# Experts' tiles in the order in which batches begin them, results added while later tiles run, and layer 0's maxima piece ahead of the scores

## What is computed

```python
xn = _layernorm(x)
x = x + _L0_attn_ref(xn, ...) + _L0_ffn_ref(xn, ...)      # 16 heads of 8, |i-j| <= 128
xn = _layernorm(x)
x = x + _L1_attn_ref(xn, ...) + _L1_ffn_ref(xn, ...)      # one head of 128; 8 experts, top 2
```

```python
scores_topk, idx = jax.lax.top_k(xn @ w_router.T, 2)
up = moe_linear(xf, ids, w_up); u, gate = jnp.split(up, 2, axis=-1)
down = moe_linear(u * silu(gate), ids, w_down)
out = jnp.sum(down.reshape(B, S, 2, D) * weights[..., None], axis=-2)
return out + skip
```

## Time and profile before

| | |
|---|---|
| median of 3 runs | 628.71 us (627.55 to 628.91) |
| the profiled execution, its own time | 624.67 us |
| its span | 622.9 us |
| PE busy | 528.2 us (85%) |
| DVE busy | 445.0 us (71%) |
| ACT busy | 359.2 us (58%) |
| POOL busy | 293.0 us (47%) |
| mean DMA rate | 98 GB/s |

### The profile page before, as it was taken

One profiled execution on the slowest core, in us unless ns is written; L12 is line 12 of the kernel. 1 busy time (PEld: TensorE's weight loads), 2 busy tenths in 40 slices (PEclk: granted clock), 3 DMA queues, 4 the chain that ended last, 5 costly groups with the idle time before them and its releaser, 6 DMA issues. The chain is left out here.

```text
span 622.9 us, 17045 instructions
## 1 busy us (share of the span) xinstructions
PE 528.2 (85%) x5698; PEld 308.3 (49%) x5698; DVE 445.0 (71%) x1868; ACT 359.2 (58%) x1073; POOL 293.0 (47%) x327
## 2 busy tenths in 40 slices
PE   5389999899998999989999669998976999999940
PEld 4124454444444444444444436655654666666630
DVE  7698898797887979878890169999881664455526
ACT  4504777767677676776677357677641444444420
POOL 6661836447164471641000026877871555555540
PEclk9555999999999999999999779999978999999985
DMA  3946073462734627246001273111121222222229
GB/s 98 185 104 136 26 170 86 120 138 67 156 74 119 139 66 161 53 121 137 21 20 26 62 258 99 42 46 49 44 87 52 65 75 75 78 75 77 79 73 359
DMA packets 50837, 60.99 MB, mean 98 GB/s; under 512 B 9905, under 2 KB 41781, under 8 KB 48960
## 3 DMA queue, kind: packets, MB, share of 16 engines
q1 hardware_dynamic: 45280, 49.34, 32.3%
q0 software_dynamic: 4320, 8.47, 4.0%
q10 hardware_dynamic: 1152, 2.10, 0.9%
HBM read 31.68 MB, written 28.39 MB: 96 GB/s over the span
## 5 line engine op out<-in xcount | busy, mean ns | idle before, releaser
L639 DVE CUSTOM_DVE_ANT_0 A<-A,band 128x320 f32<-128x320 f32 (+2 forms) x512 | 214.4, 465 | 43.8 <-PE A L801 42.7
L502 ACT ACTIVATE Pb<-SB 128x320 f32<-128x320 f32 (+2 forms) x512 | 174.9, 402 | 84.8 <-PE SB L837 82.7
L801 PE MATMUL A<-Ks,Qs 48*64 48x320 bf16 (+2 forms) x1024 | 131.3, 307 | 9.2 <-DVE mneg L639 3.7
L828 PE MATMUL SB<-Qs,Ks 50*64 50x320 bf16 (+2 forms) x1024 | 125.9, 292 | 12.6 <-ACT Pb L502 10.8
L828 PEld LDWEIGHTS SB<-Qs,Ks 50*64 50x64 bf16 x1024 | 55.8, 106 | 102.3 <-ACT Pb L502 85.2
L1577 POOL DMA_INDIRECT results<-y,xt x71 | 69.5, 979 | 62.3 <-ACT y L1591 56.6
L837 PE MATMUL SB<-ends,ident 64*64 64x64 bf16 (+1 forms) x1024 | 97.5, 205 | 0.0
L850 PE MATMUL PV<-Pb,Va 128*32 128x320 f32 (+2 forms) x1024 | 85.6, 406 | 0.4 <-ACT Pb L502 0.4
L1677 PE MATMUL l_S<-w_up,xT 128*128 x142 | 77.7, 629 | 1.4 <-ACT xT L1585 1.4
L639 DVE DVE_READ_ACCUMULATOR2_ANT mneg<- 128x1 f32 x512 | 72.7, 142 | 0.0
L1133 POOL DMA_INDIRECT expert_rows<-pay,pos x64 | 62.9, 983 | 19.4 <-issue 18.2
(11 more groups left out here) (229 smaller groups left out, 912.7 us busy)
## 6 DMA issues: line engine op xcount, KB each, us to landing
Qs<-parts_dram SPq DMA_DIRECT2D x16, 384.0 KB, 5.9
Ks<-parts_dram SPq DMA_DIRECT2D x16, 384.0 KB, 9.2
xt<-expert_rows SPq DMA_DIRECT2D x71, 65.0 KB, 1.8
yb<-results SPq DMA_DIRECT2D x8, 512.0 KB, 6.9
parts_dram<-qp SPq DMA_DIRECT2D x16, 192.0 KB, 2.9
parts_dram<-kp SPq DMA_DIRECT2D x16, 192.0 KB, 2.8
xb<-in_x SPq DMA_DIRECT2D x8, 256.0 KB, 2.8
parts_dram<-qp SPq DMA_DIRECT2D x16, 128.0 KB, 2.6
```

Of the source, the lines that this page charges most:

```text
L502: act.activation(Pb[:, group % 4, c, 0:w], SB[k % NB_BANKS][:, 0:w], ACT.Exp).then_inc(act_exp, 1)
L639: nc.vector.tensor_tensor_reduce(scores_of, scores_of, band[:, skip:skip + w], -1.0, 3e38, ALU.add, ALU.min, mneg[:, step % 2, col:col + 1 ...
L801: mm = nc.tensor.matmul(A[k % NA_BANKS][out:out + HP, 0:w], Qs[b % RING][rows, a, HP * sub:HP * sub + HP], Ks[b % RING][rows, a, lo:lo + w ...
L828: nc.tensor.matmul(out[r0:r0 + HP, 0:w], Ks[b % RING][rows, a, HP * sub:HP * sub + HP], Qs[b % RING][rows, a, lo:lo + w], start=True, stop ...
```

## The change

Three things are changed.

1. In layer 0, PE's loop issues `piece` before `scores` in every unit, and four side jobs move: `turn_xq` from u = 46 to 48 and its copy from 47 to 49, `turn_max` from 52 to 53 and its copy from 53 to 54.
2. The table of tiles orders them by the batch in which an expert's tile gets its first row, then by expert. For this PE keeps a count of each expert's rows after every batch (one more matmul of 8 columns in `rank`), DVE computes the table in 128 partitions (partition t for tile t) from 64 (batch, expert) cells, PE turns the two columns, and DVE copies them to `tab`. DVE prepares constants for it in batch 6 (`order_constants`).
3. A batch's results are loaded, added and stored while later tiles run. SP loads `yb` of batch b after `load(22 + 8 b)` for b up to 6, DVE adds it in tiles 22 + 8 b and 23 + 8 b for b up to 5, and SP stores it after `load(30 + 8 b)`. Only batch 7's load, and the adding and storing of batches 6 and 7, come after the tiles.

By count: an expert's tiles begun by batches 0 to b number at most 8 (b + 1) + 7 in all, so they lie among tiles 0 to 8 b + 14, and `load(22 + 8 b)` has waited for the results of just these.

```diff
@@ layer0, ACT @@
-                if u == 53 and b + 1 < NB:
+                if u == 54 and b + 1 < NB:
                     evac_mT(STEPS * b + 2)
...
-                    if u == 47:
+                    if u == 49:
                         evac_xqT(g)
@@ layer0, PE @@
             for u in range(SLOTS):
-                scores(b, u)
                 step, n = ahead(STEPS * b + u // UNITS, u % UNITS)
                 if step < NSTEP:
                     piece(step, n)
+                scores(b, u)
...
-                if u == 52 and b + 1 < NB:
+                if u == 53 and b + 1 < NB:
                     turn_max(STEPS * b + 2, (act_xqT, g + 1) if g < NB else (dve_x1, b))
...
-                    if u == 46:
+                    if u == 48:
                         turn_xq(g, (dve_x1, b) if b > 0 else (act_k1, g))
@@ layer1, DVE @@
+        def order_constants():
+            nc.vector.tensor_copy(tile_f[:], tile_i[:]).then_inc(dve_const, 1)
+            nc.vector.tensor_scalar(tile_row[:], tile_i[:], float(P), None, ALU.mult).then_inc(dve_const, 1)
+            nc.vector.tensor_tensor(upto[:], ..., ALU.is_le).then_inc(dve_const, 1)
...
         def tables():
...
+            step(nc.vector.tensor_tensor(more[:], now, before, ALU.subtract))
+            step(nc.vector.tensor_tensor(cprod[:], upto[:].unsqueeze(1).to_broadcast([P, NB, NE, NE]),
+                                         more[:].unsqueeze(2).to_broadcast([P, NB, NE, NE]), ALU.mult))
+            step(nc.vector.tensor_reduce(cwithin[:], cprod[:], AX.X, ALU.add), False)
...
+        def rows_of_tiles():
+            dve.wait_ge(pe_cols, 1)
+            step(nc.vector.tensor_copy(tab[:], QK[0:1, 0:2 * P].rearrange("p (c t) -> p c t", t=P)[:, :, 0:NTILES]))
...
             if not last:
                 ranks(g, last)
+            if g == NB - 2:
+                order_constants()
...
             nc.vector.tensor_tensor(x2b[:, g * NT:(g + 1) * NT, :], OU[:].rearrange("p (i d) -> p i d", i=NT),
                                     xn[g % 3][:], ALU.add).then_inc(dve_out, 1)
+        rows_of_tiles()
@@ layer1, PE @@
+            if g > 0:
+                c = CNT + NE * (g - 1)
+                mm = nc.tensor.matmul(RT[:, c:c + NE], ones[:], S[p][:], start=True, stop=True)
             mm.then_inc(pe_rank, 1)
...
+        pe.wait_ge(dve_fin, COLS)
+        pe.wait_ge(act_k, NB)
+        for c in range(2):
+            mm = nc.tensor.transpose(QK[0:1, c * P:(c + 1) * P], sums[:, c:c + 1], ident[:])
+        mm.then_inc(pe_cols, 1)
         pe.wait_ge(dve_fin, FIN)
@@ experts @@
+    READY = NE * 2 + 6
+    SUM_AT = READY
+    SENT_AT = READY + 8
...
+    def store(engine, b):
+        engine.wait_ge(dve_done, b + 1)
+        engine.dma_start(ov[b], x2b[:, b * NT:(b + 1) * NT, :].rearrange("p i d -> p (i d)")).then_inc(stored, 16)
@@ experts, SP @@
             load(t)
+            if t >= READY and (t - READY) % NE == 0:
+                results((t - READY) // NE)
+            if t >= SENT_AT and (t - SENT_AT) % NE == 0:
+                store(sp, (t - SENT_AT) // NE)
         for r in range(R):
             sp.wait_ge(dma_y[r], 16 * turns(r))
-        for b in range(NB):
-            sp.dma_start(yb[:, b].rearrange("p i k d -> p (i k d)"), yv[b]).then_inc(dma_yb[b], 16)
+        results(NB - 1)
@@ experts, ACT @@
-        for b in range(NB):
-            act.wait_ge(dve_done, b + 1)
-            act.dma_start(ov[b], ...).then_inc(stored, 16)
+        for b in range(NB - 2, NB):
+            store(act, b)
@@ experts, DVE @@
+            if t >= SUM_AT and t < SUM_AT + NE * (NB - 2):
+                if (t - SUM_AT) % NE == 0:
+                    both((t - SUM_AT) // NE)
+                if (t - SUM_AT) % NE == 1:
+                    total((t - SUM_AT) // NE)
         turned(NTILES - 1)
...
+        for b in range(NB - 2, NB):
+            both(b)
+            total(b)
```

More of the change, by code:

```diff
@@ L956 @@
 CAP = TOKENS + P
+NCELL = NB * NE
 NTILES = (TOKENS * TOPK + NE * (P - 1)) // P
@@ L1047, in layer1 @@
     padi = sb("padi", [1, NE], I32)
[L1048 to L1059 removed]
+    nt_a = sb("nt_a", [P, NCELL])
+    nt_f = sb("nt_f", [P, NB + 1, NE])
+    more = sb("more", [P, NB, NE])
+    cprod = sb("cprod", [P, NB, NE, NE])
+    cwithin = sb("cwithin", [P, NB, NE])
+    cbefore = sb("cbefore", [P, NB])
+    cum = sb("cum", [P, NB, NE])
+    back = sb("back", [P, NB, NE])
+    base = sb("base", [P, NCELL + 1])
+    bstep = sb("bstep", [P, NCELL])
+    le = sb("le", [P, NCELL])
+    steps = sb("steps", [P, 2, NCELL])
+    sums = sb("sums", [P, 2])
     Sb, XR, QK, OU = banks
     XV, RT = XR[:, 0:512], XR[:, 512 + 2 * (P + NE):1024]
+    CNT = 64
     blocks = XR[:].rearrange("p (b w) -> p b w", b=2)[:, :, 0:2 * (P + NE)].rearrange("p b (i w) -> p b i w", i=2)
@@ new lines, in tables @@
+            step(nc.vector.tensor_reduce(cwithin[:], cprod[:], AX.X, ALU.add), False)
+            step(nc.vector.tensor_reduce(cbefore[:], before, AX.X, ALU.add))
+            step(nc.vector.tensor_tensor(cum[:], cwithin[:], cbefore[:].unsqueeze(2).to_broadcast([P, NB, NE]), ALU.add))
+            step(nc.vector.tensor_tensor(back[:], now, cum[:], ALU.subtract))
+            step(nc.vector.scalar_tensor_tensor(base[:, 0:NCELL].rearrange("p (b e) -> p b e", e=NE), back[:], float(P),
+                                                ebase[:].unsqueeze(1).to_broadcast([P, NB, NE]), ALU.mult, ALU.add))
@@ L1516, in _ @@
         pe.wait_ge(act_exp, NT * NB)
-        pe.wait_ge(act_k, NB)
         pe.wait_ge(dve_rb, RB * NB)
@@ L1623, in residual, with both, total @@
             nc.vector.tensor_tensor(rows, rows, xall[:, b], ALU.add).then_inc(dve_res, 1)
+        def both(b):
+            dve.wait_ge(dma_yb[b], 16)
+            nc.vector.tensor_tensor(yb[:, b, :, 0, :], yb[:, b, :, 0, :], yb[:, b, :, 1, :], ALU.add).then_inc(dve_sum, 1)
+        def total(b):
+            rows = x2b[:, b * NT:(b + 1) * NT, :]
+            dve.wait_ge(dve_sum, b + 1)
+            dve.wait_ge(dve_res, b + 1)
+            nc.vector.tensor_tensor(rows, yb[:, b, :, 0, :], rows, ALU.add).then_inc(dve_done, 1)
         for t in range(NTILES):
@@ L1633, in dve_part @@
                 residual(t - FIRST_RES)
-        turned(NTILES - 1)
-        dve.wait_ge(dve_res, NB)
-        for b in range(NB):
-            dve.wait_ge(dma_yb[b], 16)
-            rows = x2b[:, b * NT:(b + 1) * NT, :]
-            nc.vector.tensor_tensor(yb[:, b, :, 0, :], yb[:, b, :, 0, :], yb[:, b, :, 1, :], ALU.add).then_inc(dve_sum, 1)
-            dve.wait_ge(dve_sum, b + 1)
-            nc.vector.tensor_tensor(rows, yb[:, b, :, 0, :], rows, ALU.add).then_inc(dve_done, 1)
+            if t >= SUM_AT and t < SUM_AT + NE * (NB - 2):
[3 more added lines that the diff above has]
+                    total((t - SUM_AT) // NE)
+        turned(NTILES - 1)
+        for b in range(NB - 2, NB):
+            both(b)
+            total(b)
     def pe_part(pe):
```

93 lines of the change are left out of this document (41 added, 52 removed).

## The result

| | kernel before | with the change |
|---|---|---|
| median | 628.81 us (623.52 to 631.59, 12 runs) | 625.08 us (622.32 to 629.12, 12 runs) |
| ratio, 95% interval | | 0.9945 (0.992 to 0.9969) |
| profiled execution, its own time | 624.67 us | 624.18 us |
| span | 622.9 us | 622.4 us |

What follows compares the result with a forecast made beforehand. No engine full in layer 0, PE pacing the tiles, uncovered transfers bounding the end. Terms -11.2 - 4.0 - 2.0 + 0.5 = -16.7 us: 608.0 from the profiled 624.67, 612.0 as a median; range about 604 to 620.

Steps and rivals of the forecast that it cites:

- The end: After the tiles: only batch 7's load, additions and store remain, 7.75 us instead of 18.91, a gain of 11.2 us.
- The shorter load alone: At the end: batch 7's load, with none behind it, might take 1.8 us instead of 3.90, making the gain 13.3.
- Layer 0: Layer 0: moved side jobs -4.0 us and `piece` ahead of `scores` -2.0 us.
- The moves: Layer 0: `l_x1s` is asked for later, so PE's wait at the turning of `xq` goes, 5 times 0.8, -4.0 us.
- the swap: Layer 0: `piece` ahead of `scores` shortens DVE's waits for PE, -2.0 us; upper bound 8, loss bounded by 2.
- layer 0 gives nothing: Rival, chance 0.20: in layer 0 PE's wait goes but another engine is next at once; 618.0 us.
- The slower rival: Layer 0, chance 0.05: PE's waits for DVE's maxima delay ACT's exp; at 0.04 us a unit, 20.5 us, giving 634.5.
- The table: Between layer 0 and the tiles: the new table's work is covered by about 4 us before the first tile; zero cost.
- The side effect: Before the first tile: PE idles about 2 us instead of 3.67; a higher clock could return at most 1.6, taken as 0.
- The tiles: Expert tiles: seven `yb` loads in SP's queue delay xt loads little, +0.5 us in all, bounds 0 and 5.5.
- the rival of held loads: Expert tiles, chance 0.20: xt loads wait behind `yb` and `out` in SP's queue, 5.5 us instead of 0.5; 617.0 us.
- The additions: Expert tiles: DVE's two additions of 0.69 us per batch, in two tiles, cost nothing while PE sets the pace.

Runs made afterwards that it cites:

- both_on_act: The changed kernel with the same `yb` loads and `out` stores, back to back, issued by ACT instead of SP, sum four tiles behind `yb`: 658.68 us, ratio 0.9946.
- ring_11: The changed kernel with 11 instead of 8 buffers of xt and y, `yb` three tiles later, batches 6 and 7 loaded behind the tiles: 615.33 us, ratio 0.9815.
- l0_both_only: The kernel before with only the layer 0 part: `piece` ahead of `scores` and the four side jobs moved: 657.75 us, ratio 0.9941.
- the mended kernel: The changed kernel with 11 buffers of xt and y, `yb` in four parts, stores in two halves: 645.17 us, ratio 0.9753; run again 650.18 us, 0.982.

## Why the prediction was wrong

**The end: right.** -11.2 forecast, 11.2 found, and 7.55 us from the last load for 7.75. The shorter load alone, kept as an end of the range, was not seen: 3.70 us with nothing behind it, for 3.90.

**Layer 0: right in sum, wrong in its parts.** -6.0 forecast; the seven batches gave 4.3 to 6.8 in the traces of all kernels with both edits, 5.5 in the one with nothing else. The moves gave 5.3 for the 4.0 put on them, the swap 0.2 beside them for 2.0, with a spread of 2.5 us on each; that the sum came out at 5.5 for 6.0 is in part luck. The first batch's start comes on top: the first `l_x1s` starts anywhere from 117.6 to 124.1 us in kernels with the same layer 0. The granted clock in 60 to 64 us does not sort them: it was 0.97 and 1.00 for 117.6 and 117.8 and 0.50 for 123.3 and 123.9, but 0.50 for 118.9 and 0.93 for 124.1 too. The rival "layer 0 gives nothing" falls. The slower rival, each wait of PE for DVE delaying ACT, had its mechanism (69 us of PEld's waits for DVE instead of 11) and no price.

**The table: hidden, as forecast.** It is ready at 461.4 us, well ahead of the first load of xt at 468.66. The side effect that I guessed, a shorter idle time of PE, went the other way: 4.40 us instead of 3.67, since the matmuls of `l_OU` took 3.84 us and not 6.74. Tiles 0 to 4 were slower by 1.2 us:

```profile
470.56 0.30 PE L1704 MATMUL l_QK<-l_ident,xt 128*128 128x128 f32 x1 [4.40 <-DMA xt<-expert_rows]
471.54 2.07 PE L1733 MATMUL l_S<-w_up,xT 128*128 x2 [0.68 <-ACT xT L1633]
```

**The tiles: the step that failed.** "+0.5 us for all seven", bounds 0 and 5.5, became +14.9, of which 13.1 from tile 22 on. Four things were wrong in the step. It let `yb` keep the DMA engines for 1.6 us, mostly drained by the next load: with a store behind it, it landed 4.5 to 5.9 us after its issue. It asked whether a load of xt would be late *behind `yb` in SP's queue*, and both_on_act shows the queue to be without effect. It priced lateness once per pair, at 2.4 us less a cover of 1.5, and so even the rival of held loads came to 5.5 us. And it left out the chain in the loop: load t waits for the scatter of tile t - 8 to land. The trace before had this chain in sight, since SP waited for scatters at nearly every load (35 times from 524 to 600 us), so a scatter that lands late at once makes a load late, and uses up the same 1.5 us of cover as the load's own lateness. Transfers of 768 KB back to back lengthened one such step from 2.98 to 5.89 us. The DMA share of 28%, on which the room for them rested, is a mean: while a pair drains it is 0.96. The additions themselves cost nothing, as forecast: DVE did not wait for `yb` in the tiles. Nor did the forecast have a term for the clock inside the stretch of tiles, which fell behind PE's wait of 2.09 us and took 1.6 us.

The sum of the forecast with the measured tiles, -16.7 - 0.5 + 14.9 = -2.3, is what was seen within the spread: medians 3.7 us apart, spans 0.5.

The Trainium skill's rule (page "DMA: Bandwidth & Descriptors", section "Queues, rings and completion order") that engines go round between queues, so that stores from ACT would have had their own turn, was set beside the rival of held loads. As I read it there, both_on_act would have won most of the 13 us back. It won nothing. That does not contradict the rule, only my use of it: by the shares of 0.96 and 0.78 the transfers compete for the time of the DMA engines, and another queue leaves that the same. For the size of the last load the page's estimate, 3.2 us, is further from the 3.70 found than the 3.90 taken from the trace.

**Open.** How the remaining lateness splits between xt's own landing and that of the scatters, since a longer ring gives slack to both. Whether the size of the parts or their spacing mends it. And what holds PE for up to 0.7 us behind a pair in ring_11, where it waits for no load.

## What to carry to other kernels

Room on the DMA engines has to be read over the time that a single transfer takes, not over a stage: here a big transfer moved into a loop delayed the small ones beside it, from either queue. Follow the loop's own buffer chain (here load, tile, scatter, load) and ask how late each link may be before you price the move; then cut the big transfers into parts, one to a tile, keep a store from following a load at once, and give the ring more buffers. Here that turned a change worth 0.2 to 0.6% into one worth 1.8 to 2.5%.

## What the runs showed of the hardware

- Splitting and spreading mattered and the queue did not: 512 KB and 256 KB right behind it from SP or from ACT, 95.0 and 94.9 us for tiles 22 to 70; the store 1.0 to 2.2 us ahead of the load instead, 86.4; parts of 128 KB spread over the tiles, 84.8.
- A load of 512 KB landed after 3.7 us alone, and after 4.5 to 5.9 us with a store of 256 KB right behind it.
- The chips of the later comparisons needed 150 to 158 us for the stage between layer 0 and the tiles, for which the first needed 118. In the trace of l0_both_only waits are put down to a releaser that the trace calls remote, which are none of the large ones before:

```profile
DVE l_mneg L1406 <- remote: 18.9, 12, 3.6
DVE x2b L1429 <- remote: 16.6, 5, 5.0
ACT l_xnT L1177 <- remote: 16.1, 5, 4.0
```

  What it is was not tried. The ratios agree within their intervals: 0.9945 and 0.9978 for the change, 0.9753 and 0.982 for the mended kernel.
- The clock after idle time: with PE idle for 0 to 1.37 us ahead of the first turning tiles 0 to 4 took 6.8 to 7.0 us in nine traces and 8.3 in one (at 1.10 us). After 2.26 to 4.56 us they took 8.4 to 10.9 in seven. In the change the granted clock was 0.53 in 471 to 475 us and 0.62 in the next 4. Among the tiles it was 0.53 in 594 to 596 us, behind a wait of PE of 2.09 us.
